# The last stage of a four-layer network: image pairs in three tiles of 128 channels, centring as a product, factors by log and exp, all transfers on SyncE's queue

## The reference, cut to what matters

```python
def _ln_cf(x, w, b, eps=1e-05):
    mu = x.mean(1, keepdims=True)
    var = ((x - mu) ** 2).mean(1, keepdims=True)
    return (x - mu) / jnp.sqrt(var + eps) * w[None, :, None, None] + b[None, :, None, None]
...
y = _ln_cf(y, out_norm_w, out_norm_b)
y = y * jax.nn.silu(z)
out = jnp.einsum('cd,bdhw->bchw', out_proj_w, y)
return x + out
```

## Time and profile before

| | us |
|---|---|
| median of 3 executions | 6007.73 |
| lowest, highest | 5997.26, 6012.96 |
| the profiled execution | 6004.98 |
| its span, first to last instruction | 6003.3 |
| first instruction of the last stage (SyncE, line 3303) | 5763.79 |

### The profile page before, as it was taken

How to read it: one execution, slowest core, us unless ns; L and a number is a source line. 1 busy time by engine, 2 the same in 40 slices (tenths; PEclk the granted TensorE clock), 3 DMA queues, 4 the chain that set the end, 5 groups by cost and what they waited for, 6 DMA issues and landing times. The chain is left out here.

```text
span 6003.3 us, 86146 instructions
## 1 busy us (share of the span) xinstructions
PE 5214.9 (87%) x34466; PEld 2382.9 (40%) x34466; DVE 4239.1 (71%) x4999; ACT 2806.1 (47%) x3970; POOL 866.9 (14%) x920
## 2 busy tenths in 40 slices
PE   7799999999889959968868899969678888888877
PEld 2355555555534424445534333323233333333323
DVE  3477767767511112278878499958889999999978
ACT  1144444444422213245521455526577777877733
POOL 1000000000000011122243000001133333333300
PEclk9899999999999979989989999979889999999989
DMA  6512112111031133344433001013210001000045
GB/s 213 135 34 40 29 34 41 26 37 28 9 95 67 53 94 130 114 142 134 134 122 122 24 28 37 23 61 107 82 38 28 6 27 36 5 28 6 14 119 150
DMA packets 299763, 398.20 MB, mean 66 GB/s; under 512 B 157980, under 2 KB 275924, under 8 KB 296108
## 3 DMA queue, kind: packets, MB, share of 16 engines
q1 hardware_dynamic: 265068, 269.58, 16.3%
q0 software_dynamic: 24608, 107.12, 5.2%
q10 hardware_dynamic: 9696, 16.07, 0.9%
HBM read 226.19 MB, written 166.50 MB: 65 GB/s over the span
## 5 line engine op out<-in xcount | busy, mean ns | idle before, releaser
L3767 DVE TENSOR_TENSOR_SCAN s_h<-s_da,s_h 128x448 f32<-128x448 f32 x672 | 732.8, 1134 | 0.6 <-ACT s_da L3694 0.4
L3614 PE MATMUL s_py<-s_prod,s_idf 128*128 128x448 f32 x1344 | 585.9, 559 | 22.3 <-ACT s_ycol L3707 21.0
L622 PE MATMUL b_pc<-b_ca,b_wdm 128*113 128x392 f32 x1152 | 487.2, 520 | 31.3 <-DVE b_wdm L837 25.5
L3694 ACT ACTIVATE s_da<-s_dt,s_al 128x448 f32<-128x448 f32 x672 | 405.6, 657 | 197.5 <-DVE s_h L3767 147.1
L765 ACT ACTIVATE b_band<-b_psel 124x784 f32<-124x784 f32 x264 | 217.7, 824 | 427.3 <-PE b_psel L690 424.3
L622 PE MATMUL b_pc<-b_cb,b_wdm 128*113 128x392 f32 x960 | 401.9, 518 | 0.0
L3752 DVE TENSOR_TENSOR s_h<-s_dtu,s_pb 128x896 f32<-128x896 f32 x336 | 358.2, 1066 | 28.1 <-POOL s_dtu L3801 22.2
L2812 DVE SCALAR_TENSOR_TENSOR j_zc<-j_zt,j_gw,j_zc 128x896 f32<-128x896 f32 x336 | 361.4, 1145 | 6.7 <-ACT j_zt L2753 6.7
L3774 DVE TENSOR_TENSOR s_prod<-s_h,s_pc 128x896 f32<-128x896 f32 x336 | 363.9, 1083 | 0.1
L3614 PEld LDWEIGHTS s_py<-s_prod,s_idf 128*128 128x128 f32 x1344 | 249.4, 193 | 218.1 <-issue 167.4
L3790 POOL TENSOR_TENSOR s_dt<-s_dt,s_dtu 128x448 f32<-128x448 f32 x168 | 249.5, 1485 | 460.8 <-DVE s_h L3767 425.8
(11 more groups left out here) (672 smaller groups left out, 11277.5 us busy)
## 6 DMA issues: line engine op xcount, KB each, us to landing
b_qk<-mid_qkvp SPq DMA_DIRECT2D x96, 240.2 KB
d_vt<-mid_vd SPq DMA_DIRECT2D x200, 96.0 KB
d_qs<-mid_qd SPq DMA_DIRECT2D x20, 744.0 KB, 5.0
d_ks<-mid_kd SPq DMA_DIRECT2D x20, 744.0 KB, 7.8
b_v<-mid_qkvp SPq DMA_DIRECT2D x6, 1922.0 KB
mid_pout<-d_out POOLq DMA_DIRECT2D x20, 558.0 KB, 4.2
mid_qkvp<-a_out SPq DMA_DIRECT2D x42, 248.0 KB, 2.3
mid_qkvp<-a_out ACTq DMA_DIRECT2D x42, 248.0 KB, 2.2
```

The lines of the kernel that those rows point to most:

```text
L622: mm = pe.matmul(pc[n % 2][0:113, 0:392], wdm[:, slot, p, 0:113], src, start=(w == STARTS[a]), stop=(w + 1 == STARTS[a + 1]))
L3614: mm = pe.matmul(y, idf[:, :], prod[j % 3][:, e, :], start=(pr == 0 and e == 0), stop=False)
L3694: last = a.activation(da[j % 4][:, e, :], dt[s % 2][:, span(c)], ACT.Exp, scale=al[:, u, n:n + 1])
L3767: v.tensor_tensor_scan(x, along(da[j % 4][:, e, :]), x, before_, ALU.mult, ALU.add).then_inc(scanned, 1)
```

## The change

The stage now works on image pairs: a step is one chunk of 448 positions of two images, a tile of 128 partitions x 3 x 448, and there are 14 steps, all written out. The mean is not computed by itself: one set of products with "identity minus 1/192" writes the centred tile, which ScalarE copies out and squares from PSUM. The variance comes out on all three tiles, and the factor is exp(-0.5 log(var + eps)) on ScalarE instead of a root there and a reciprocal on VectorE. The scaled tile then gets scale and shift, gate, mixing and residual; the residual sum is written in place into the buffer of the loaded x3. Stores are issued by SyncE, in line with the loads; four small loads go to ScalarE's queue. GpSimd has nothing left to do. In the removed lines (in full above) only "..." stands.

```diff
--- before.py
+++ after.py
@@ -3254,183 +3254,247 @@
+def scan_outputs(nc, x3, ys, zs, on_w, on_b, out_wT, ident, out):
...
+        NY, NZ, NX = 4, 4, 6
...
+        yin = [sb(f"h_yin{i}", [128, 3, CH]) for i in range(NY)]
+        zin = [sb(f"h_zin{i}", [128, 3, CH]) for i in range(NZ)]
+        xin = [sb(f"h_xin{i}", [128, 3, CH]) for i in range(NX)]
+        ce = [sb(f"h_ce{i}", [128, 3, CH]) for i in range(2)]
+        sq = sb("h_sq", [128, 3, CH])
+        rs = [sb(f"h_rs{i}", [128, 3, CH]) for i in range(2)]
+        yn = [sb(f"h_yn{i}", [128, 3, CH]) for i in range(3)]
+        pA, pV = pt("h_pa", 3), pt("h_pv", 3)
...
+        xo = paired(out.rearrange("b c h w -> (b c) (h w)"))
...
         @block.sync
         def _(sp):
...
+            def load_y(s):
+                if s >= NY:
+                    sp.wait_ge(centred, s - NY + 1)
+                sp.dma_start(yin[s % NY][:, :, :], paired(ys)[s // NCH, :, :, span(s)]).then_inc(y_loaded[s % NY], 16)
+            def load_zx(s):
+                if s >= NZ:
+                    sp.wait_ge(gated, s - NZ + 1)
+                sp.dma_start(zin[s % NZ][:, :, :], paired(zs)[s // NCH, :, :, span(s)]).then_inc(z_loaded[s % NZ], 16)
+                if s >= NX:
+                    sp.wait_ge(stored[s % NX], 16 * (s // NX))
+                sp.dma_start(xin[s % NX][:, :, :], paired(x3)[s // NCH, :, :, span(s)]).then_inc(x_loaded[s % NX], 16)
+            def store(s):
+                sp.wait_ge(finished, 3 * (s + 1))
+                sp.dma_start(xo[s // NCH, :, :, span(s)], xin[s % NX][:, :, :]).then_inc(stored[s % NX], 16)
+            load_y(0)
+            load_y(1)
+            load_y(2)
+            load_zx(0)
+            for s in range(LAST + 2):
+                if live(s + 3):
+                    load_y(s + 3)
+                if live(s + 1):
+                    load_zx(s + 1)
+                if live(s - 3):
+                    store(s - 3)
...
         @block.tensor
         def _(pe):
...
+            pe.wait_ge(consts, 3)
+            def channels(dst, src, full, half, rest):
+                pe.matmul(dst[:, 0, 0:CH], full[:, :], src[:, 0, :], start=True, stop=False)
+                pe.matmul(dst[:, 1, 0:CH], half[:, :], src[:, 1, :], start=True, stop=False)
+                pe.matmul(dst[:, 2, 0:CH], full[:, :], src[:, 2, :], start=True, stop=False)
+                pe.matmul(dst[:, 0, 0:CH], rest[lo, :], src[lo, 1, :], start=False, stop=True)
+                pe.matmul(dst[:, 2, 0:CH], rest[hi, :], src[hi, 1, :], start=False, stop=True)
+                pe.matmul(dst[lo, 1, 0:CH], rest[:, lo], src[:, 0, :], start=False, stop=True)
+                return pe.matmul(dst[hi, 1, 0:CH], rest[:, hi], src[:, 2, :], start=False, stop=True)
+            def centre(s):
+                pe.wait_ge(y_loaded[s % NY], 16 * (s // NY + 1))
+                if s:
+                    pe.wait_ge(copied, s)
+                    pe.wait_ge(squared, s)
+                channels(pA, yin[s % NY], keep, keep1, drop).then_inc(centred, 1)
+            def spread(s):
+                pe.wait_ge(squared, s + 1)
+                if s:
+                    pe.wait_ge(log_done, s)
+                channels(pV, sq, m192, m192h, m192).then_inc(spread_done, 1)
+            def project(s):
+                x = yn[s % 3]
+                if s == 0:
+                    pe.wait_ge(wide_ready, 2)
+                pe.wait_ge(gated, s + 1)
+                pe.wait_ge(finished, 3 * s)
+                pe.matmul(pO[0][:, 0, 0:CH], w[:, 0, 0:128], x[:, 0, :], start=True, stop=False)
+                pe.matmul(pO[1][:, 0, 0:CH], w[:, 2, 64:192], x[:, 2, :], start=True, stop=False)
+                pe.matmul(pO[0][:, 0, 0:CH], w[lo, 1, 0:128], x[lo, 1, :], start=False, stop=True)
+                pe.matmul(pO[1][:, 0, 0:CH], w[hi, 1, 64:192], x[hi, 1, :], start=False, stop=True).then_inc(mixed, 2)
+            def project_odd(s):
+                x = yn[s % 3]
+                pe.wait_ge(finished, 3 * s + 1)
+                pe.matmul(pO[0][:, 0, 0:CH], wd[:, :], x[:, 1, :], start=True, stop=False)
+                pe.matmul(pO[0][lo, 0, 0:CH], w[:, 0, 128:192], x[:, 0, :], start=False, stop=True)
+                pe.matmul(pO[0][hi, 0, 0:CH], w[:, 2, 0:64], x[:, 2, :], start=False, stop=True).then_inc(mixed, 1)
+            for s in range(LAST + 1):
+                if live(s):
+                    centre(s)
+                if live(s - 2):
+                    project(s - 2)
+                if live(s):
+                    spread(s)
+                if live(s - 2):
+                    project_odd(s - 2)
         @block.scalar
         def _(a):
...
+            a.dma_start(idf[:, :], ident).then_inc(idf_loaded, 16)
+            a.dma_start(w[:, :, :], out_wT.rearrange("(t p) o -> p t o", p=128)).then_inc(par_loaded, 16)
...
+            a.preload_act_table_set("natural_log_exp_and_others")
+            def square(s):
+                a.wait_ge(centred, s + 1)
+                if s >= 2:
+                    a.wait_ge(normed, s - 1)
+                a.activation(ce[s % 2][:, :, :], pA[:, :, 0:CH], ACT.Copy).then_inc(copied, 1)
+                if s:
+                    a.wait_ge(spread_done, s)
+                a.activation(sq[:, :, :], pA[:, :, 0:CH], ACT.Square).then_inc(squared, 1)
+            def root(s):
+                a.wait_ge(spread_done, s + 1)
+                if s >= 2:
+                    a.wait_ge(normed, s - 1)
+                a.activation(rs[s % 2][:, :, :], pV[:, :, 0:CH], ACT.Ln, bias=EPS).then_inc(log_done, 1)
+                a.wait_ge(log_done, s + 1)
+                a.activation(rs[s % 2][:, :, :], rs[s % 2][:, :, :], ACT.Exp, scale=-0.5).then_inc(rstd_ready, 1)
+            def affine(s):
+                if s == 0:
+                    a.wait_ge(vec_loaded, 32)
+                a.wait_ge(normed, s + 1)
+                for t in range(3):
+                    x = yn[s % 3][:, t, :]
+                    last = a.activation(x, x, ACT.Identity, bias=ob[:, t:t + 1], scale=og[:, t:t + 1])
+                last.then_inc(affine_done, 1)
+            for s in range(LAST + 1):
+                if live(s):
+                    square(s)
+                if live(s - 1):
+                    affine(s - 1)
+                if live(s):
+                    root(s)
         @block.vector
         def _(v):
...
+            v.tensor_scalar(keep[:, :], idf[:, :], -1.0 / C, None, ALU.add)
+            v.tensor_scalar(keep1[lo, lo], idf[lo, lo], -1.0 / C, None, ALU.add)
+            v.tensor_scalar(keep1[hi, hi], idf[hi, hi], -1.0 / C, None, ALU.add).then_inc(consts, 1)
+            v.wait_ge(par_loaded, 16)
+            v.tensor_copy(wd[lo, lo], w[lo, 1, 128:192]).then_inc(wide_ready, 1)
+            v.tensor_copy(wd[hi, hi], w[hi, 1, 0:64]).then_inc(wide_ready, 1)
+            def normal(s):
+                v.wait_ge(rstd_ready, s + 1)
+                v.wait_ge(copied, s + 1)
+                if s >= 3:
+                    v.wait_ge(mixed, 3 * (s - 2))
+                v.tensor_tensor(yn[s % 3][:, :, :], ce[s % 2][:, :, :], rs[s % 2][:, :, :], ALU.mult).then_inc(normed, 1)
+            def gate(s):
+                v.wait_ge(z_loaded[s % NZ], 16 * (s // NZ + 1))
+                v.wait_ge(affine_done, s + 1)
+                y = yn[s % 3][:, :, :]
+                v.tensor_tensor(y, y, zin[s % NZ][:, :, :], ALU.mult).then_inc(gated, 1)
+            def finish(s, t):
+                if t == 0:
+                    v.wait_ge(x_loaded[s % NX], 16 * (s // NX + 1))
+                v.wait_ge(mixed, 3 * s + (2, 3, 2)[t])
+                x = xin[s % NX][:, t, :]
+                v.tensor_tensor(x, pO[0 if t < 2 else 1][:, 0, 0:CH], x, ALU.add).then_inc(finished, 1)
+            for s in range(LAST + 1):
+                if live(s - 1):
+                    normal(s - 1)
+                if live(s - 2):
+                    finish(s - 2, 0)
+                    finish(s - 2, 2)
+                if live(s - 1):
+                    gate(s - 1)
+                if live(s - 2):
+                    finish(s - 2, 1)
...
+    scan_outputs(nc, s["x3"], s["ys"], s["zs"], a["on_w"], a["on_b"], a["out_wT"], a["ident"], out)
...
+        on_w=twice(l3["out_norm_w"]), on_b=twice(l3["out_norm_b"]), out_wT=two(l3["out_proj_w"].T),
```

More of the change, by code:

```diff
@@ L3283, in scan_outputs @@
+        z_loaded = [sem(f"h_z_loaded{i}") for i in range(NZ)]
+        x_loaded = [sem(f"h_x_loaded{i}") for i in range(NX)]
         centred = sem("h_centred")
+        copied = sem("h_copied")
         squared = sem("h_squared")
-        var_done = sem("h_var")
-        std_done = sem("h_std")
-        rstd_done = sem("h_rstd")
+        spread_done = sem("h_spread")
+        log_done = sem("h_log")
+        rstd_ready = sem("h_rstd")
         normed = sem("h_normed")
-        affine = sem("h_affine")
+        affine_done = sem("h_affine")
@@ L3300, in _, with live, span @@
+        LAST = NS2 + 2
```

(39 more changed lines are left out.)

111 lines of the change are left out of this document (19 added, 92 removed).

## The result

The changed kernel takes 5966.3 us (median of 4 runs, 5964.68 to 5969.46), the kernel before 6004.15 beside it: a ratio of 0.9939 (95% interval 0.9927 to 0.9951), a gain of 37.9 us where 27 were forecast. Of the 14.7 us between 5981 and the result, 3.6 are the kernel before itself, whose median fell from 6007.73 to 6004.15 with one more run; the other 11 are the gain.

The account below looks back on a forecast made before the run. VectorE, with the reciprocal largest, was taken to set the pace, TensorE next. TensorE's start, 25.3, twelve steps of 13.2 and an end of 22.0 + 2.7 gave 5976.0, 27.3 us less; median forecast 5981 us, range 5972 to 5995.

Parts of the forecast that it names:

- TensorE's start, into the stage: Last stage: TensorE starts at 5769.4 as before, when the first ys tile has landed.
- from there to the end of the second variance: Pipeline fill: low-clock centring, first variance and a second step without mixing take 25.3 us, to 5794.7.
- step: TensorE's 4.3 centring, 4.3 variance, 2.65 and 1.85 mixing, plus a 0.1 stall: 13.2 us, against 14.56 before.
- last variance to last residual: Stage end: log and exp, scaling, affine, gate, mixing and residuals take 14.9 us, plus 0.2 of waits.
- low clock at the end: TensorE idling in gaps up to 2 us at the end costs 2.7 us, from between 0 and 4.5.
- last residual to end: Stage end: the last store is issued and lands, the stage ending behind it, 6.9 us.
- 22.0 + 2.7: From the last variance's end at 5951.3: 22.0 us at full clock plus 2.7 for low clock, ending at 5976.0.
- a cheaper VectorE alone could gain little more than that: Kernel before, last stage: TensorE already waits only 1.11 us for variance, which limits a VectorE-only gain.
- that rival: TensorE's six pairs run one after the other: 4.5 us more a step, 63 in all, 6044 us; chance 4%.
- the rival in which every change empties the array: TensorE: 0.17 us more per change of shape, 1.7 a step, gain only 3 us, 6004; chance 3%.
- SyncE's order: Stores in line with loads costed at nothing; rival: they hold loads back, step 14.6 us or more, 6008 to 6020; 2%.
- The transfers: Last stage DMA share expected near 0.8; rival that transfers set the pace: gain 0 to 3 us, 6006; chance 6%.

Follow-up runs that it names:

- (a): The changed kernel with its stores issued by GpSimd again instead of SyncE: 5975.06 us, ratio 0.9956.
- (b): The kernel before with only its stores moved into SyncE's order, behind each pass's loads: 6002.93 us, ratio 0.9997.
- (j): The kernel before with log and exp for root and reciprocal, and stores on SyncE's queue: 5971.34 us, ratio 0.9942.
- (i): g with products reordered so equal array shapes stand together, five changes of shape a step instead of eight: 5925.82 us, ratio 0.9868.
- g: The changed kernel with variance and mean in four products each, mean subtracted on VectorE, third PSUM tile for mixing: 5927.14 us, ratio 0.9887.
- (d): The changed kernel with root and reciprocal in place of log and exp: 5998.77 us, ratio 0.9989.
- (e): The changed kernel with the four pairs of centring and variance as eight whole zero-padded products: 5997.44 us, ratio 0.9997.
- (h): The changed kernel with its 21 products reordered so equal shapes stand together, six changes of shape instead of ten: 5969.71 us, ratio 0.9938.
- (c): The kernel before with only log and exp in place of root and reciprocal: 5962.98 us, ratio 0.9932.

## Why the prediction was wrong, point by point

The direction and the sum of the new step held; the size of the gain did not, nor did the weight given to the parts of the change. By the prediction's own steps, in us (gain over the forecast in the last column):

| step | forecast | measured | more gain |
|---|---|---|---|
| start of the stage | 5763.79 | 5762.43 | 1.4 |
| TensorE's start, into the stage | 5.65 | 4.69 | 1.0 |
| from there to the end of the second variance | 25.3 | 25.6 | -0.3 |
| step | 13.2 | 13.12 | 1.0 (twelve) |
| last variance to last residual | 15.1 | 15.05 | 0 |
| low clock at the end | 2.7 | none | 2.7 |
| last residual to end | 6.9 | 4.3 | 2.6 |

Together 8.4: the 35.7 of the span against 27.3. The medians show 37.9; the 2.2 more are scatter between a median and one profiled execution.

**The step that failed** is the end, "22.0 + 2.7", in two terms. *The 6.9 us* were taken from the row of a store that GpSimd issues, although the change gives that store to SyncE. (a) shows what the 2.6 us consist of: 1.9 are the engine that issues the store, and 0.7 that the same end takes 6.2 and not 6.9 us with GpSimd too; (b) shows the same in the kernel before (3.3). The queue was costed where it could do harm and not where it helped. *The 2.7 us* for the low clock rested on gaps of up to 2 us. The gaps before the last products were 0.82 and 0.80, and both ran at 1.02 or less a pair of records, the high level. Over the ends of all kernels, products that ran at the high level before a gap of 0.8 to 2.2 us kept it behind the gap ((j) 3.22 us for eight records behind 1.85, (i) 1.02 for two behind 2.20), and those behind 2.58 (g, 1.86 for two), 3.25 and 7.80 (d) ran at the low one. Once the level was low, a short gap did not tell what came next: behind 0.80 us the kernel before was back at the high level (3.22 for eight), behind 0.81 (b) was not (6.16 for eight), nor was (d) behind 0.82 (1.83 for two). So the forecast was right to call the clock the unknown of the end. Its gaps of up to 2 us came out at 0.82 and 0.80, and even those of 1.85 and 2.20 in (j) and (i) left the level high. *TensorE's start* was tied to the first tile of ys; with ys first in the queue it waits for the matrices instead (h_keep), 1.0 us earlier. The 1.4 at the start of the stage is scatter of the stages ahead.

**The range** was too narrow on the good side. It allowed the end no better value than the forecast's less the clock, and counted 5 us for scatter where the starts of the stage alone differ by 11.

**Wrong in the reasoning, though not in the number:** "a cheaper VectorE alone could gain little more than that", the 1.11 us of TensorE's wait. As a number a step it holds: a step without the reciprocal takes 6.01 instead of 7.28, 1.27 less. What it is worth was missed: 28 times 1.27 is 36 us, all of the change's gain. By the prediction's own numbers it was 28 x 1.11 = 31 us, more than the 27 forecast for the whole change; I called it little without multiplying it out. Nor were there 7.35 us of VectorE work in a step: records overlap, and 57.1 of 60 us are 6.9 in 7.28. What sets the 7.28 is a chain that comes back to VectorE, and three rows of the kernel before show the part of it that the prediction left out:

```profile
5895.10 0.95 ACT L3386 ACTIVATE h_sq<-h_ce 96x896 f32<-96x896 f32 x1 [2.66 <-DVE h_ce L3412]
...
5897.89 0.54 ACT L3390 ACTIVATE h_rs<-h_pv 96x448 f32<-96x448 f32 x1 [1.83 <-PE h_pv L3364]
...
5898.46 2.95 DVE L3404 RECIPROCAL h_rs<-h_rs 96x448 f32<-96x448 f32 x1 [0.33 <-ACT h_rs L3390]
```

Centring (5894.05), squares (5895.10), variance (5896.10), root (5897.89), reciprocal (5898.46) and the next centring (5901.33) each start within 0.1 us of the end of the one before. The reciprocal is 2.95 us of this chain of 7.28. Without it TensorE's products set the pace instead, at 6.01.

**Right:** 13.1 us of TensorE's slots a step; a pair takes one slot, so that rival falls, (e) giving its price; a change of shape costs 0.1 on either side, as (h) and (i) confirm, and not the 0.17 more of the rival in which every change empties the array. The Trainium skill, page TensorEngine Tiling (Array Packing), section Key Properties, says that the array drains on a change of mode. The traces here agree that a change costs, and put it at 0.19 us; whether the array drains in that time they do not show. The chain at start and end held within 0.3 us. SyncE's order holds nothing back: the waits of TensorE in the stage are these, none of them for a transfer; of the 13.4 us 4.7 lie in the stage, the one for h_pv is of the first two steps, those for h_xin of the last:

```profile
PE h_pa L3358 <- DVE h_keep L3463: 13.4, 1, 13.4
PE h_pv L3358 <- ACT h_sq L3423: 5.1, 2, 2.6
PE h_po L3385 <- DVE h_xin L3486: 1.6, 2, 0.8
PE h_po L3393 <- DVE h_xin L3486: 1.6, 2, 0.8
```

**The transfers** did not set the pace, by far: 211 GB/s took a share of 0.60, where the prediction looked for nearly 0.8.

## What to carry to other kernels

Before trusting an estimate for a large change, price its smallest part alone in the same unit (us a step times steps): here one instruction of 2.95 us on VectorE, replaced by one more on ScalarE, which was busy 23.5 of 60 us, was worth the whole of the change, and the layout that came with it cost 1.1 us in the time of two old steps. When a second engine is nearly as busy as the first, count its slots (whole products, pairs, changes of shape) and cut those: going from 15 to 11, and then placing equal shapes side by side, took the stage from 205.2 to 157.6 us. And compare stages, and better still steps, not totals, where untouched stages scatter by more than the edit is worth.

## What the runs showed that was not expected

**Tiles on 128 partitions, twice as large, move more bytes for the same busy share.** With loads alone the changed kernel moved 389 GB/s at a share of 1.06, the kernel before 255 at 1.08. The same holds when the step is steady, and for either queue: 96 partitions gave 190 at 0.72, 191 at 0.74 (b), 228 at 0.85 (c) and at 0.89 (j), some 255 to 270 GB/s at a full share; 128 partitions gave 211 at 0.60, 219 at 0.63 (a), 184 at 0.53 (d) and 285 at 0.81 (g, from 5840 to 5860), some 350. The two stand about as 96 to 128. The layout also doubled the size of a transfer, and no run parted the two.

**The last store is cheaper from SyncE**: 3.9 to 4.4 us from the last residual to the end in nine kernels, against 6.2 to 7.25 from GpSimd in three. In (a) and (b) the engine that waits for the store to land moved along with the one that issues it, so what part each has is not shown.

**The reciprocal** takes 8.54 us for 1344 elements a partition and 2.95 for 448, 6.4 to 6.6 ns each, where the product of two such tiles takes 1.56 for 1344. Log and exp together take 2.6 for the same tile.
